# A two-layer cross-attention: first-layer keys and queries block by block in turn, attention slots filled four heads at a time, loads issued before any wait, first row maxima taken inside VectorE's chain

## The reference

```python
# layer 0: text = first 77 context rows, ip = the other 435
q, k, v = heads(x @ Wq.T), heads(text @ Wk.T), heads(text @ Wv.T)
k_ip, v_ip = heads(ip @ Wk_ip.T), heads(ip @ Wv_ip.T)
out = softmax(q k^T / 4) v + softmax(q k_ip^T / 4) v_ip
x = out @ Wo.T + bo + x
# layer 1: text = first 508 context rows, ip = the last 4
q, k_t, v_t = heads(x @ W_q), heads(text @ W_k), heads(text @ W_v)
probs_t = softmax(q k_t^T / 4)
qsem = l2norm(probs_t @ text)                      # per head, 512 wide
fused = q k_ip^T / 4 + 0.5 * qsem l2norm(ip)^T
out = probs_t v_t + softmax(fused) * spatial_mask * v_ip
x = out @ W_out + b_out + x
```

## Time and profile before

| | |
|---|---|
| time, median of 3 runs | 1737.86 us (1735.75 to 1742.17) |
| profiled execution | 1735.92 us, its span 1734.1 us |
| granted TensorE clock, mean | 0.987 |
| TensorE busy | 1589.0 us, 92% |
| VectorE busy | 1273.5 us, 73% |
| ScalarE busy | 1114.1 us, 64% |
| GpSimd busy | 461.9 us, 27% |
| HBM read, written | 41.49 MB, 34.10 MB |

### The profile page before, as it was taken

The page is one execution under the profiler, slowest core; times in us unless marked ns, Lnnn a source line. Parts: engine busy times, 40 slices in busy tenths (PEclk is TensorE's granted clock), DMA queues, the critical chain, the costliest instruction groups (busy, mean ns, idle before and its releaser), DMA issues.

```text
span 1734.1 us, 32461 instructions
## 1 busy us (share of the span) xinstructions
PE 1589.0 (92%) x8608; PEld 1211.7 (70%) x8608; DVE 1273.5 (73%) x3548; ACT 1114.1 (64%) x2323; POOL 461.9 (27%) x1225
## 2 busy tenths in 40 slices
PE   5688999999988899999998889999999889999993
PEld 2455379999655448999945546999965554899991
DVE  2489358888778837888679854888877883688875
ACT  1499267777279736777539945777735992677760
POOL 0144023332034302323204411333202440223320
PEclk9899999999999999999999999999999999999997
DMA  7310130000311031001041113000022103000000
GB/s 205 112 36 28 59 100 19 19 21 22 106 42 36 15 109 59 18 18 33 2 124 37 36 55 99 20 21 19 25 61 78 36 23 97 27 19 18 19 20 15
DMA packets 50908, 82.83 MB, mean 48 GB/s; under 512 B 8064, under 2 KB 15504, under 8 KB 50832
## 3 DMA queue, kind: packets, MB, share of 16 engines
q1 hardware_dynamic: 48160, 76.78, 14.3%
q10 hardware_dynamic: 2672, 5.13, 0.8%
HBM read 41.49 MB, written 34.10 MB: 44 GB/s over the span
## 4 chain that ended last, share of the span: by engine, by line
PE 76%; ACT 12%; issue 5%; SPq 5%; DVE 2%; DMA 0%; ACTq 0%; POOL 0%; DVEq 0%
PE ps_w L930 45%; PE ps_t L930 11%; PE ps_s L930 11%; PE ps_b L930 7%; ACT probsT_high L513 5%; ACT probsT L521 4%; SPq L343 2%; PE ps_m L930 1%; SPq L336 1%; DVE row_max L724 1%; ACT probs L532 1%; SPq L308 1%; ACT q_slot L506 1%; DMA q_slot<-probsT_low 0%; ACT probs L609 0%
## 5 line engine op out<-in xcount | busy, mean ns | idle before, releaser
L513 ACT ACTIVATE probsT_high<-ps_t 128x512 fp32r<-128x512 f32 x640 | 382.5, 598 | 116.6 <-PE ps_t L930 112.8
L705 DVE TENSOR_TENSOR probsT_low<-probsT,probsT_high 128x512 fp32r<-128x512 f32 x560 | 395.2, 706 | 77.3 <-ACT probsT L521 68.5
L930 PE MATMUL ps_w<-gram,probsT_high 128*128 128x416 f32 (+2 forms) x1280 | 387.5, 314 | 0.0
L521 ACT ACTIVATE probsT<-ps_t 128x512 f32<-128x512 f32 x640 | 384.0, 600 | 0.0
L930 PE MATMUL ps_w<-gram_low,probsT_high 128*128 128x384 f32 (+2 forms) x1280 | 351.5, 303 | 0.0
L444 POOL TENSOR_SCALAR exp_bias<-row_max 128x1 f32<-128x1 f32 x320 | 127.7, 399 | 686.9 <-DVE row_max L763 686.9
L549 ACT ACTIVATE probs<-ps_s,exp_bias 128x508 f32<-128x508 f32 x320 | 220.6, 690 | 122.6 <-POOL exp_bias L444 79.2
L930 PE MATMUL ps_t<-q_slot,k_slot 98*128 98x512 f32 x640 | 258.7, 422 | 1.4 <-ACT probsT L521 0.5
L930 PE MATMUL ps_s<-k_slot,q_slot 96*128 96x512 f32 x640 | 237.9, 414 | 19.5 <-DMA q_slot<-probsT_low 15.1
L930 PEld LDWEIGHTS ps_w<-gram_low,probsT_high 128*128 128x128 f32 (+1 forms) x1280 | 242.3, 189 | 11.0
L930 PEld LDWEIGHTS ps_w<-gram,probsT_high 128*128 128x128 f32 (+1 forms) x1280 | 240.8, 188 | 11.5
(11 more groups left out here) (165 smaller groups left out, 2031.2 us busy)
## 6 DMA issues: line engine op xcount, KB each, us to landing
parts_k<-probsT_high SPq DMA_DIRECT2D x48, 256.0 KB, 2.7
q_slot<-parts_q SPq DMA_DIRECT2D x128, 96.0 KB
k_slot<-parts_k SPq DMA_DIRECT2D x128, 96.0 KB
parts_q<-probsT_low SPq DMA_DIRECT2D x24, 256.0 KB, 2.6
parts_q<-x_sb SPq DMA_DIRECT2D x16, 256.0 KB, 2.5
k_slot<-probsT_high SPq DMA_DIRECT2D x96, 32.0 KB
parts_k<-probsT_high SPq DMA_DIRECT2D x24, 128.0 KB, 2.8
ctx_sb<-in_ctxT ACTq DMA_DIRECT2D x3, 1024.0 KB, 5.6
```

The lines of the kernel that those rows point to most:

```text
L513: nc.scalar.activation(probsT_high[1 - par][:, t, :], ps_t[:, t % 2, :], ACT.Exp, scale=SCALE)
L521: nc.scalar.activation(probsT[:, t, :], ps_t[:, t % 2, :], ACT.Exp, scale=SCALE).then_inc(pt_block[l], 1)
L705: nc.vector.tensor_tensor(probsT_low[1 - par][:, t, :], probsT[:, t, :], probsT_high[1 - par][:, t, :].bitcast(F32), ALU.subtract).then_in ...
L930: return nc.tensor.matmul(out, lhsT, rhs, start=start, stop=stop)
```

## The change

- In the making of k0 and q0 the blocks alternate: k0 block 0, q0 block 0, k0 block 1, and so on, on TensorE, ScalarE, VectorE and SP alike. k1 and q1 keep their order.
- The four slots of queries become one tile `q_slots` (98 rows, 4 slots, 512), those of keys `k_slots`. The columns of six weight matrices are permuted on the host so that the four heads of a group lie interleaved in the first 64 rows of a block; then one DMA fills a part of all four slots. `first_heads` issues 3 DMAs a name instead of 12, with a semaphore of their own, `first_in`; TensorE waits for all six at the first filling step.
- `store` issues two DMAs a block instead of three; one of them writes the doubled part twice. The scratch is laid out by group: the rows of one head are four rows apart.
- At the start the loads go out ahead of SP's wait for the constants; the row of the key slots is one DMA behind the first nine; the weights for later are in another order; biases and mask are issued after the slot loads of the first layer. TensorE's waits for constants move behind `queries_keys0`, its wait for `weights_in` to the keys of layer 1. GpSimd gets eight memsets of one column that give the slot semaphores a starting credit.
- At a change of batch, VectorE takes the first maxima of the next batch inside its chain, after the third of four products, no longer after the chain.

The diff, cut to its core:

```diff
-STORES = CBN * 3 * 16
+ROW_TARGETS = {"q": ((0, 1), (2,)), "k": ((0, 2), (1,))}
+STORES = CBN * 2 * 16
...
+    [(name, m, "D") for m in range(CBN) for name in ("k0", "q0")]
...
+HIGHS = [(name, m) for name in ("k1", "q1") for m in range(CBN)] + [(name, m) for m in range(CBN) for name in ("k0", "q0")]
...
+RING_NEXT = {("k0", 0): 2, ("q0", 0): 3, ("k0", 1): 0, ("q0", 1): 1, ("k0", 2): 2, ("q0", 2): 3}
+RING_BEFORE = {("k0", 2): ("k0", 0), ("q0", 2): ("q0", 0)}
...
+        scratch = {n: nc.dram_tensor(f"parts_{n}", [3, TURNS, D, SLOTS, S], F32, kind="Internal").ap()
...
-            sp.wait_ge(ip_shift_in, 1)
-            for slot in k_slot:
-                sp.dma_start(slot[ALL_ROWS - 1:ALL_ROWS, :].bitcast(F32), ip_shift[:, :]).then_inc(k_rows_in, 16)
             load_ctx(sp, 0)
...
-            for n, src in (("k1", wk1), ("ki1", wki1), ("v1", wv1), ("vi1", wvi1)):
+            sp.wait_ge(ip_shift_in, 1)
+            sp.dma_start(k_slots[ALL_ROWS - 1:ALL_ROWS, :, :].bitcast(F32),
+                         ip_shift[:, :].unsqueeze(1).to_broadcast([1, SLOTS, T])).then_inc(k_rows_in, 16)
+            for n, src in (("k1", wk1), ("ki1", wki1)):
...
-            for n, src in (("o0", wo0), ("q1", wq1), ("o1", wo1)):
-                load_small(n, src, weights_in)
...
-            sp.dma_start(mask_sb[:, :], mask).then_inc(weights_in, 16)
+            load_small("o0", wo0, weights_in)
+            load_small("q1", wq1, weights_in)
+            for n, src in (("v1", wv1), ("vi1", wvi1)):
+                load_big(n, src, weights_in)
+            load_small("o1", wo1, weights_in)
...
+            def load_biases():
+                for l, src in ((0, bo0), (1, bo1)):
+                    for m in range(CBN):
+                        sp.dma_start(bias_o[l][0:CB[m], m:m + 1], src[m * P:m * P + CB[m], :]).then_inc(weights_in, 16)
+                sp.dma_start(mask_sb[:, :], mask).then_inc(weights_in, 16)
...
+                rows = scratch[name].rearrange("i g d k s -> (g d k) i s")[P * m:P * m + CB[m], :, :]
+                for part, at in enumerate(ROW_TARGETS[name[0]]):
+                    src = parts[name][part].bitcast(F32)[0:CB[m], m, :]
+                    dst = rows[:, at[0]:at[-1] + 1:max(at[-1] - at[0], 1), :]
+                    sp.dma_start(dst, src.unsqueeze(1).to_broadcast([CB[m], len(at), S])).then_inc(stored[name], 16)
+
+            def first_heads(l, name):
+
+                slots = q_slots if name[0] == "q" else k_slots
                 for i, part in enumerate(ROW_PARTS[name[0]]):
-                    dst = scratch[name][i, :, :, :].rearrange("h d s -> (h d) s")[P * m:P * m + CB[m], :]
-                    sp.dma_start(dst, parts[name][part].bitcast(F32)[0:CB[m], m, :]).then_inc(stored[name], 16)
...
-            def first_heads(l, name):
...
-                for k in range(SLOTS):
-                    slot = (q_slot if name[0] == "q" else k_slot)[k]
-                    for i, part in enumerate(ROW_PARTS[name[0]]):
-                        sp.dma_start(slot[PART * i:PART * i + PART, :].bitcast(F32),
-                                     parts[name][part].bitcast(F32)[D * k:D * k + D, 0, :]).then_inc(slots_in[l][k], 16)
...
+                    sp.dma_start(slots[PART * i:PART * i + PART, :, :].bitcast(F32),
+                                 parts[name][part].bitcast(F32)[0:D * SLOTS, 0, :]).then_inc(first_in[l], 16)
+
+            def load_slots(b, l, turn, k):
...
+                used = HEADS * b + SLOTS * (turn - 1) + k + 1
                 sp.wait_ge(pt_block[l], TB * used + CREDIT1)
                 for slot, src in ((q_slot[k], scratch[f"q{l}"]), (k_slot[k], scratch[f"k{l}"])):
-                    sp.dma_start(slot[0:SCORE_ROWS, :].bitcast(F32), src[:, n, :, :])\
+                    sp.dma_start(slot[0:SCORE_ROWS, :].bitcast(F32), src[:, turn, :, k, :])\
...
-                for name in names:
-                    for m in range(CBN):
-                        wait_freed(sp, b, name, m)
-                        sp.sem_inc(passed, 1)
-                        if m == 0:
-                            first_heads(l, name)
-                        store(name, m)
+                for name, m in [job for job in HIGHS if job[0] in names]:
+                    wait_freed(sp, b, name, m)
+                    sp.sem_inc(passed, 1)
+                    if m == 0:
+                        first_heads(l, name)
+                    store(name, m)
...
             split_and_loaded(FIRST, 0, 0, ("k0", "q0"))
+            load_biases()
...
+            for i in range(2 * SLOTS):
+                nc.gpsimd.memset(out_all[:, 2 + i:3 + i], 0.0).then_inc(slots_in[i // SLOTS][i % SLOTS], CREDIT)
...
                 if ahead:
-                    high(b, "k0", 1)
-                    high(b, "k0", 2)
+                    high(b, "q0", 0)
                 act.wait_ge(ask_exp, b + 1)
                 nc.scalar.activation(fused[:, :, :], fused[:, :, :], ACT.Exp).then_inc(exp_in, 1)
                 if ahead:
-                    highs(b, "q0")
+                    for name, m in HIGHS[2 * CBN + 2:]:
+                        high(b, name, m)
...
+            def maxima0(b, head, half, par=0):
+
+                cs = slice(2 * half, 2 * half + 2)
+                dve.wait_ge(s_half, 2 * (HEADS * b + head) + half + 1)
+                nc.vector.tensor_reduce(out=row_max[0][par][:, cs, 0:1], in_=ps_s[:, :, 0:TEXT0], axis=AX.X, op=ALU.max)
+                nc.vector.tensor_reduce(out=row_max[0][par][:, cs, SHIFT_ROWS - 1:SHIFT_ROWS], in_=ps_s[:, :, TEXT0:T],
+                                        axis=AX.X, op=ALU.max).then_inc(max_half, 1)
...
-                if scores:
-                    maxima(0)
+                if scores and (use or transposed or last is FIRST):
+                    maxima0(b, n + 2, 0, par)
...
+                if ahead:
+                    low(b, "q0", 0)
                 nc.vector.tensor_tensor(wide[0], o1[:, :, V1:V1 + D], rz.to_broadcast([P, nd, D]), ALU.mult)
                 if ahead:
                     low(b, "k0", 1)
-                    low(b, "k0", 2)
...
                     if ahead and i < 2:
-                        for m in ((0,), (1, 2))[i]:
-                            low(b, "q0", m)
+                        for job in ((("q0", 1),), (("k0", 2), ("q0", 2)))[i]:
+                            low(b, *job)
+                    if ahead and i == 2:
+                        maxima0(b + 1, 0, 0)
                     link(b, last)
...
-            pe.wait_ge(built, 1)
-            pe.wait_ge(ident_r_in, 1)
-            pe.wait_ge(dve_consts_in, 1)
-            pe.wait_ge(k_rows_in, 16 * SLOTS)
...
+                if first:
+                    pe.wait_ge(first_in[0], FIRST_LOADS * (b + 1))
+                    wait_freed(pe, last, "q0", 1)
+                if second:
+                    wait_freed(pe, last, "q0", 2)
...
+                if first:
+                    pe.wait_ge(first_in[1], FIRST_LOADS * (b + 1))
...
+                for m in range(CBN):
+                    keys(b, "k0", "ki0", TEXT0, (m,))
+                    if m == 0:
+                        pe.wait_ge(x_in, 32 * batch + 32)
+                        if b is FIRST:
+                            pe.wait_ge(weights0_in["q"], 32)
+                    by_channels(b, "q0", "q0", x_sb, (m,))
...
+                pe.wait_ge(weights_in, WEIGHTS)
                 keys(b, "k1", "ki1", TEXT1)
...
             queries_keys0(FIRST, 0)
+            pe.wait_ge(built, 1)
+            pe.wait_ge(dve_consts_in, 1)
+            pe.wait_ge(ident_r_in, 1)
+            pe.wait_ge(k_rows_in, 16)
             fill0(step0, 0)
-            pe.wait_ge(weights_in, WEIGHTS)
...
+    for name in ("wq0", "wk0", "wki0", "wq1", "wk1", "wki1"):
+        w = given[name]
+        given[name] = w.reshape(-1, TURNS, SLOTS, D).transpose(0, 1, 3, 2).reshape(-1, C)
```

49 lines of the change are left out of this document (14 added, 35 removed).

## The result

The changed kernel takes 1713.72 us (median of 4 runs, 1711.14 to 1719.4); the kernel before, beside it, 1736.8. The ratio is 0.9859, with a 95% interval of 0.984 to 0.9878. The forecast was 1707.1, range 1703 to 1718. The profiled executions are 1735.92 before and 1711.14 after: 24.8 us gained, where the sum said 28.8. The median lies another 2.6 above the profiled run; what is known of how runs differ stands further down.

What follows compares the result with a forecast made beforehand. TensorE bounds the kernel (76% of the span); the change touches only the stretches between head loops. 21.9 at the start plus 6.9 at changes of batch, 28.8, from 1735.92 gives 1707.1 us; range 1703 to 1718.

Steps and rivals of the forecast that it cites:

- (a): Start: loads issued at 0.7 instead of 11.38, 10.7 us earlier; first matmul at 10.6, queries ended at 32.5.
- (b): Start: slots filled four at a time, biases late; first scores at 33.9, second half at 45.0, 21.9 us saved.
- the bounds: Start: first scores not before 32.5 (TensorE busy) and not after 35.5 (landing time behind a full queue).
- my first rival: Start: slot DMAs into 16 partitions slow, first scores at 35.5, clock probably drops, 4.6 us; 1711.7, chance 0.25.
- a sign of being wrong: Start: first scores after 36 with the clock at 0.50 would show the forecast wrong.
- (c): Changes of batch: query slots are in before TensorE asks, so its waits go; 6.9 us saved over three changes.
- (d): Changes of batch: first maxima inside VectorE's chain delay its end by 1.37 us, covered; cost zero, gain zero.
- the cover: Changes of batch: VectorE's chain ends 0.15 us before TensorE asks for it, by up to 0.9 more.
- (e): Changes of layer: three DMAs of 128 KB land by 216.6, before TensorE asks at 216.91; cost zero.
- (f): Stores and first layer's biases: merged stores and late biases are in before anything waits for them; zero.
- The last two rivals: Start: loads don't start earlier, 1716.4, chance 0.05. Loops: slot loads from regrouped scratch slower, 1777, chance 0.03.

Runs made afterwards that it cites:

- The late weights: The change with the second layer's weights loaded behind the first heads' slots and stores instead of ahead of them: 1715.15 us, ratio 0.986.

## Why the prediction was right, and where it was off

*(a) Loads early: right.* First matmul at 10.29 (10.6). The queries ended at 33.5, not 32.5: the first key block took 7.2 us, and 5.6 before, from the 21.28 of the earlier trace rows to the second block:

```profile
26.86 1.01 PE L930 MATMUL ps_t<-ctx_sb,w_k 128*128 128x77 f32 x8
```

I had shifted a duration along with its start. The three kernels with useless work ahead do this block in 3.8 to 4.0 us, so the slowness comes of standing still before it. Without such work it took 6.1 to 7.2 us in the nine traces that start at 10.2 to 10.7, and 5.6 and 5.7 in the two that start later. What sets the size stays open.

*(b) First scores: inside the bounds, at their upper end.* 35.39 against 33.9 and at most 35.5. The step that was off is the queue's rate: 4.1 us for slots and stores at 381 GB/s. The windows of the change show the DMA engines full all through, with less than that in two places behind the issue of the slots:

```profile
28.00:30.00 2.00, 2.00 (x7) 0.80 (x6) 0.61 (x1) 0.00 (x0) 0.00 (x0) 1.00 1.06 168
...
32.00:34.00 2.00, 1.49 (x4) 0.19 (x2) 0.19 (x1) 0.47 (x1) 0.00 (x0) 1.00 1.07 234
```

Up to 33 us all transfers together moved 10.1 MB (306 GB/s on average), which my sum had moved by 31.7. So the place of my first rival (0.25) was right and its price not: after 1.89 us of standing still the clock held. That was luck: with the same code up to there, TensorE stood 2.34, 2.70 and 4.87 us in three other kernels' profiled runs, and the clock fell in all three. Their first scores came at 35.22 to 37.20, the last past my bound of 35.5 and past the 36 with a fallen clock that I had named as a sign of being wrong. The late weights show that the wait was not necessary at all.

What I didn't see is 50 to 58 us. I asked for the clock only where TensorE waits for a DMA, and it can also fall in a thinly filled pipeline: 1.45 us.

*(c) Changes of batch: right, mis-sized.* 8.1 us against 6.9. The waits went, and the nine groups became 0.42 shorter in each, which I had put at zero ("TensorE's work is the same"). Undoing the order alone gave the wait back, at twice its size, and the clock was lost with it.

*(d) Maxima in the chain: right.* Zero within 0.1 us; the cover was 1.07 us, at the upper end of "0.15 us, and by up to 0.9 more". One reading behind it was wrong: before, VectorE waited for ScalarE three times in that chain, not only for 0.91 us. The other two:

```profile
449.25 0.69 DVE L699 TENSOR_TENSOR probsT_high<-ps_t,probsT_high 128x512 fp32r<-128x512 f32 x1 [1.01 <-ACT probsT_high L500]
450.77 0.18 DVE L869 RECIPROCAL rip<-root 128x4 f32<-128x4 f32 x1 [0.82 <-ACT root L633]
```

*(e) Changes of layer: wrong.* Cost 1.1 us each, put at zero. I charged 96 KB more to the last DMA at 211 GB/s. But the scores now wait for all three, 384 KB, where they had waited for the 96 KB of slot 0: 288 KB more. As an estimate, at the 127 to 164 GB/s of the two full windows that is 2.0 us, against 0.8 of slack before. The stores, which my sum left out here, are in the same windows, so how the 2.0 divide between slots and stores stays open. The Trainium skill, page SBUF — State Buffer, section on the DMA port swizzle, has 104 GB/s for 16 partitions. No run here gives the rate of such a DMA alone, and the 0.1 to 0.2 that I drew from the page has the same fault in the bytes.

*(f) Stores and biases: right.* No wait for either. The last two rivals are out as well: the loads did start earlier, and the loops of layer 0, which read the regrouped scratch, have no wait for a DMA and moved by 0.22 us at most.

The terms that were off add up: 2.9 at the start, 2.9 at the changes of layer, less 1.2 at the changes of batch and 0.5 in the loops, is 4.1, against the 4.0 between 28.8 and 24.8. The range held, for a reason that was only partly in it. The median lies 2.6 us above the profiled run, and the change's other runs have no trace; their mean clocks (0.990, 0.986 and 0.990 against 0.991) point at the clock, and the places where kernels with the same code lost it are the first scores, the changes of layer and the end. That is argued, not shown. The 4.0 between sum and profiled run came out of one run with luck at the start.

## What to carry to other kernels

When a small transfer is merged into a large one, charge the whole set's bytes, look at what is issued right behind it, and ask whether the consumer needs only the first piece: three merged DMAs cost 1.1 us at each change of layer, where twelve small ones in order of need cost nothing. Loads that nobody needs for 130 us belong behind the ones that TensorE is about to ask for. A gain of 4 us can vanish in the clock: compare traces stretch by stretch, with the granted clock beside each, before calling an edit worthless. And before believing a gain of a few us in one stretch, look at how far that stretch moves between kernels that have the same code there.
